# Three queues of a Mamba-like layer put in another order: SiLUs, squares and splits on ScalarE, GpSimd and VectorE

## What is computed

```python
proj = x @ Win.T                       # x is layer-normed
x_ssm, z, Bm, Cm, dt_raw = ...         # H*P, H*P, H*N, H*N, H columns
dt = softplus(dt_raw + dt_bias)
xc, Bc, Cc = (silu(causal_conv(u, w)) for u, w in ((x_ssm, wx), (Bm, wb), (Cm, wc)))
decay = exp(dt * -exp(A_log))
# for each token t: h = decay_t * h + (dt_t * xc_t) outer B_t;  y_t = h @ C_t
y = y * rsqrt(mean(y * y, axis=-1) + 1e-06)     # by head
y = y * silu(z)
return y.reshape(B, T, H * P) @ Wout.T
```

## Time and profile before

| | |
|---|---|
| median of three runs | 1110.2 us |
| the profiled execution | 1114.78 us |
| its span on the core | 1113.4 us |
| TensorE busy, matmuls | 1049.8 us (94%) |
| TensorE busy, weight loads | 870.7 us (78%) |
| VectorE busy | 777.2 us (70%) |
| GpSimd busy | 701.3 us (63%) |
| ScalarE busy | 610.5 us (55%) |
| granted TensorE clock, mean | 0.976 |

### The profile page before, as it was taken

One profiled execution on the slowest core, in us unless ns is written; L12 is line 12 of the kernel. 1 busy time (PEld: TensorE's weight loads), 2 busy tenths in 40 slices (PEclk: granted clock), 3 DMA queues, 4 the chain that ended last, 5 costly groups with the idle time before them and its releaser, 6 DMA issues.

```text
span 1113.4 us, 23878 instructions
## 1 busy us (share of the span) xinstructions
PE 1049.8 (94%) x9902; PEld 870.7 (78%) x9902; DVE 777.2 (70%) x1178; ACT 610.5 (55%) x945; POOL 701.3 (63%) x692
## 2 busy tenths in 40 slices
PE   8899999999999999999989999998888889999998
PEld 6678888888888888888877888886654578788887
DVE  5688887888878889788857446556758844655554
ACT  5877787777777767686715222225943533322221
POOL 3866786787867878676863667544447352365553
PEclk9999999999999999999999999999999979999999
DMA  3312111111111112101020643302131120233311
GB/s 108 109 68 77 48 61 64 60 57 67 58 49 67 53 63 73 41 32 48 1 68 3 227 134 101 118 1 67 43 94 28 29 64 3 94 129 100 121 65 39
DMA packets 47218, 75.97 MB, mean 68 GB/s; under 512 B 11330, under 2 KB 34150, under 8 KB 47110
## 3 DMA queue, kind: packets, MB, share of 16 engines
q1 hardware_dynamic: 47110, 74.44, 20.8%
HBM read 68.13 MB, written 2.36 MB: 63 GB/s over the span
## 4 chain that ended last, share of the span: by engine, by line
PE 63%; DVE 22%; ACT 6%; POOL 4%; issue 3%; DMA 1%; SPq 0%; DVEq 0%; POOLq 0%; ACTq 0%
PE psum L675 33%; PE psum L912 9%; DVE arena L1659 9%; PE psum L647 4%; DVE arena L1696 3%; PE psum L808 3%; PE psum L763 3%; PE psum L755 2%; PE psum L1021 2%; ACT arena L1201 1%; PE psum L985 1%; DVE arena L1919 1%; PE psum L1049 1%; PE psum L1033 1%; DMA vT<-arena 1%
## 5 line engine op out<-in xcount | busy, mean ns | idle before, releaser
L675 PE MATMUL psum<-vT,split 128*128 128x512 f32 x2136 | 542.7, 404 | 10.2 <-DVE arena L1659 5.5
L675 PEld LDWEIGHTS psum<-vT,split 128*128 128x128 f32 x2136 | 394.1, 191 | 100.9 <-DVE arena L1659 7.2
L1659 DVE SCALAR_TENSOR_TENSOR arena<-psum,arena 128x1023 f32<-128x1023 f32 (+2 forms) x208 | 265.6, 1277 | 80.5 <-ACT arena L1201 59.2
L2099 POOL TENSOR_TENSOR split<-arena,split 128x256 fp32r<-128x256 f32 x178 | 132.7, 759 | 65.1 <-ACT split L1126 64.9
L1201 ACT ACTIVATE arena<-psum,arena 128x512 f32<-128x512 f32 x160 | 109.4, 691 | 99.1 <-PE psum L675 98.2
L2306 POOL TENSOR_TENSOR arena<-arena,bcast 128x512 f32<-128x512 f32 x64 | 84.3, 1318 | 113.8 <-ACT arena L1370 97.3
L1370 ACT ACTIVATE arena<-psum,arena 128x512 f32<-128x512 f32 x72 | 49.7, 690 | 177.3 <-PE psum L675 177.2
L1809 DVE SCALAR_TENSOR_TENSOR arena<-psum,arena 128x512 f32<-128x512 f32 x72 | 53.9, 749 | 122.3 <-POOL arena L2306 117.3
L912 PEld LDWEIGHTS psum<-split_down,split_hid 128*128 128x128 f32 x864 | 114.9, 195 | 9.8 <-DVE split_hid L1822 3.2
L912 PE MATMUL psum<-split_down,split_hid 128*128 128x256 f32 x864 | 117.9, 287 | 2.5 <-DVE split_hid L1822 2.5
L2126 POOL TENSOR_TENSOR arena<-arena,v 128x1021 f32<-128x1021 f32 x32 | 76.4, 2389 | 46.9 <-DVE arena L1659 46.9
(11 more groups left out here) (217 smaller groups left out, 1540.2 us busy)
## 6 DMA issues: line engine op xcount, KB each, us to landing
bcast<-scratch_a SPq DMA_DIRECT2D x32, 512.0 KB, 3.6
bcast<-scratch_e SPq DMA_DIRECT2D x32, 512.0 KB, 4.2
arena<-in_w_a SPq DMA_DIRECT2D x16, 768.0 KB, 4.4
arena<-in_wg SPq DMA_DIRECT2D x36, 128.0 KB, 3.6
arena<-in_wu SPq DMA_DIRECT2D x36, 128.0 KB, 3.5
arena<-in_wd SPq DMA_DIRECT2D x36, 128.0 KB, 3.9
arena<-in_wout_a SPq DMA_DIRECT2D x8, 256.0 KB, 2.6
vT<-arena SPq DMA_DIRECT2D x2, 1024.0 KB, 5.3
```

Of the source, the lines that this page charges most:

```text
L675: m = pe.matmul(bank, split[:, t % SPLITS, i, q, :], vT[:, j, q, half * BANK:(half + 1) * BANK], start=(n == 0), stop=(n == 3 * KD - 1))
L1659: dve.scalar_tensor_tensor(out=tile[:, s:T], in0=bank[:, 0:T - s], scalar=cw_a[:, j, i, TAPS - 1 - s:TAPS - s], in1=tile[:, s:T], op0=ALU. ...
L2099: pool.tensor_tensor(split[:, t % SPLITS, 1], raw, split[:, t % SPLITS, 0].bitcast(F32), ALU.subtract).then_inc(sem["split"], 1)
```

## The change

Nothing is added or taken away; instructions move within three queues, all in the loop of layer (a).

ScalarE, body j: `silu(j, 4)`, which stood behind `first_tap(nxt, 0)` of body j, now stands at the end of the body before, as `silu(nxt, CONV - 1)`. `silu(nxt, 3)` moves ahead of `gate(nxt)`. `square(j)` stands at the end of body j, where `square(j - 1)` stood in the middle of body j. In odd bodies from 3 on, `gated_hi(j - 2)` stands ahead of `turned(j, 1, 1)`, and `wout_hi` ahead of `project_to(2)`. `silu(nxt, 0)` stands ahead of `turned(j, 1, 1)`. In body 0 the exponentials of `carries` come after `first_tap(1, 1)` and `silu(1, 0)` and not first.

VectorE: `sum_squares(j - 1)` stands after `mask(j, 0, 1)` and ahead of `taps(2, 1, 2)`, where it stood after `mask(j, 1, 1)`.

GpSimd: in odd bodies from 3 on, `wout_lo` stands right after `gated_lo`, ahead of `light(nxt, 1)` and the split of `project_to(2)`, where it stood behind them.

```diff
@@ ScalarE, scalar_program, first_layer @@
                             weights(TILES_A * nxt + i + SPLITS - 1)
                             first_tap(nxt, i)
-
-                    def silu_to(i):
-                        if nxt < PAIRS:
-                            silu(nxt, i)
-
-                    if j == 0:
-                        carries("a")
+                            if i in (2, 3):
+                                silu(nxt, i - 1)
+
                     project_to(0)
-                    if j:
-                        silu(j, CONV - 1)
                     turned(j, 0, 0)
                     turned(j, 0, 1)
                     turned(j, 1, 0)
-                    project_to(1)
+                    if nxt < PAIRS:
+                        weights(TILES_A * nxt + SPLITS)
+                        first_tap(nxt, 1)
+                    if j >= 3 and j % 2 == 1:
+                        gated_hi(j - 2)
+                    if nxt < PAIRS:
+                        silu(nxt, 0)
                     if j == 0:
+                        carries("a")
                         decays(0)
                     turned(j, 1, 1)
-                    if j >= 2:
+                    if j >= 2 and j % 2 == 0:
                         gated_hi(j - 2)
-                    silu_to(0)
-                    project_to(2)
-                    if j:
-                        square(j - 1)
                     if j >= 3 and j % 2 == 1:
                         wout_hi((j - 3) // 2)
-                    silu_to(1)
+                    project_to(2)
                     project_to(3)
-                    silu_to(2)
                     project_to(4)
                     if nxt < PAIRS:
                         decays(nxt)
                         weights(TILES_A * nxt + CONV + SPLITS - 1)
+                        silu(nxt, CONV - 2)
                         gate(nxt)
-                        silu(nxt, CONV - 2)
-                for g in range(2):
-                    square_head(PAIRS - 1, g)
+                        silu(nxt, CONV - 1)
+                        square(j)
+                    else:
+                        square_head(j, 0)
+                        square_head(j, 1)
@@ VectorE, vector_program, first_layer @@
                     mask(j, 0, 0)
                     mask(j, 0, 1)
+                    sum_squares(j - 1)
                     taps(2, 1, 2)
                     carry(j, range(0, 3))
                     taps(2, 3)
...
                     mask(j, 1, 0)
                     taps(3, 1)
                     mask(j, 1, 1)
-                    sum_squares(j - 1)
                     taps(3, 2)
@@ GpSimd, gpsimd_program, first_layer @@
                     if j >= 3 and j % 2 == 1:
                         gated_lo(j - 2)
+                        wout_lo((j - 3) // 2)
                     if nxt < PAIRS:
                         light(nxt, 1)
                     project_to(2)
-                    if j >= 3 and j % 2 == 1:
-                        wout_lo((j - 3) // 2)
```

## The result

Six runs of the changed kernel beside six of the kernel before gave a median of **1118.15 us** (1114.28 to 1119.98) against 1110.49; the ratio is 1.0056, with a 95% interval from 1.0028 to 1.0084. Twelve more runs beside another 29 of the kernel before gave 1116.65 against 1111.98, ratio 1.0032 (1.0010 to 1.0054). So the change costs 5 to 8 us in the medians.

A forecast was written before the change was run, and what follows sets the result against it. The prediction took TensorE to set the pace of the first layer's loop; 1.6 + 2.6 + 5 x 1.0 - 2.5 = +6.7 us, against a median of 1110.2, gave 1116.9 us, 0.6% more. The range was 1104 to 1124.

The forecast's parts named there:

- body 0: First loop body: carried products come 0 to 2.4 us later, but TensorE waits 2.40 us for VectorE soon after: zero.
- body 1: Second loop body: silu(1, 4) and square(0) add 1.9 us ahead of the first tap, the sum 1.1; net +1.6 us.
- bodies 2 and 3: Early loop bodies: no idle time before taps(2) in body 2, first tap 2.8 us late in body 3; together +2.6 us.
- last body: Body 15: TensorE's 2.87 us wait for normalize(14) goes, about 0.4 is lost again; gain 2.5 us.
- The odd bodies: Bodies 5, 7, 9, 11, 13: late first tap and early sum delay taps(2), so TensorE reaches inside(j, 0) 1.0 us later each.
- ScalarE's tail: End of a body: silu(nxt, 3) waits for light ahead of the gate; an odd body's first tap comes 1.4 us later.
- Even bodies: Loop's even bodies: first tap 0.9 to 1.8 us late, mostly taken in; the sum fits VectorE's idle 1.84 us; zero.
- rival 2: Even bodies at taps(2) pay too, up to 1.1 us in six bodies from 4 on; 1123.5 us; chance 0.15.
- rival 1: Odd bodies absorb the delay and only the gains stay, -5.5 us; 1104.7 us; chance 0.20.
- The sum's early place: End of body 8: GpSimd's normalize, no longer waiting for the sum, and light(9, 3) behind it end 1.4 us earlier.

The follow-up runs named there:

- e2: Kernel before with only VectorE's sum_squares(j - 1) early, behind mask(j, 0, 1), and ScalarE's square(j) at the body's end; 1114.26 us, ratio 1.0028.
- e5: Changed kernel with VectorE's taps(2, 3) moved behind all seven steps of the carry; 1107.53 us, ratio 0.9957 to the kernel before.
- e3: Changed kernel with sum_squares(j - 1) early only in even bodies from 4 on and the last body; 1111.16 us, ratio 1.0002 to the kernel before.
- e7: Changed kernel with sum_squares(j - 1) back behind mask(j, 1, 1) and gate(nxt) again ahead of silu(nxt, 3); 1118.10 us, ratio 1.0050 to the kernel before.
- e1: Changed kernel with only sum_squares(j - 1) put back behind mask(j, 1, 1); 1125.72 us, ratio 1.0135 to the kernel before.
- e9: Changed kernel with a second, unused 1.21 us reduction ahead of sum_squares(j - 1) in even bodies 4 to 14; 1118.35 us, ratio 1.0054 to the kernel before.
- e8: Kernel before with only body 0's two exponentials of ScalarE's carries moved after silu(1, 0); 1111.55 us, ratio 1.0001.
- e4: Kernel before with late carries in body 0, and sum_squares(j - 1) early in even bodies from 4 on and the last; 1102.10 us, ratio 0.9934.
- e6: Kernel before with late body-0 carries, early sum in even bodies from 4 and the last, taps(2, 3) behind the carry; 1099.94 and 1098.22 us.

## Why the prediction was right

| step | predicted | first traces | second traces |
|---|---|---|---|
| body 0, to the start of body 1 | 0 | -0.8 | -2.3 |
| body 1 | +1.6 | +1.4 | +1.4 |
| bodies 2 and 3, to `inside(3, 0)` | +2.6 | +2.5 | +2.5 |
| from there to the start of body 15 | +5.0 | +3.8 | +3.8 |
| last body | -2.5 | -3.4 | -3.3 |
| sum | +6.7 | +3.5 | +2.2 |

**The odd bodies.** The mechanism was the right one. The sum alone (e2) costs 0.87 in an odd body, the wait stands where it was put, even bodies stay at 0.53, and shortening the chain by 1.2 us takes 1.2 us off the wait (e5). Each odd body, with the tail before it, came to 0.83 us instead of 1.0. Five times that less the 0.3 at the end of body 14, which the sum had not counted, is the 3.8. The prediction's own terms give 1.1 and not 1.0 (1.42 of lateness less 1.24 and 0.15 of idle time, and 1.1 for the sum), so this term was too high by 0.3 each and not by 0.2.

**Bodies 1 to 3.** All three wait 1.4 us for the carry instead of 0.5. In body 3 the first tap comes 2.8 us late, counted from the start of body 2 (37.24 us behind it for 34.46), as worked out. What idle time doesn't take in stands not only at the carry, where the prediction had it: body 3 waits 0.53 us for `scale_u` and loses 0.3 ahead of product 2, and body 1 loses 0.28 and 0.3 there. The sizes (1.4 for 1.6, 2.5 for 2.6) came out right all the same.

**ScalarE's tail.** silu(nxt, 3) ahead of the gate does wait for `light` and the first tap is 1.7 us later against the transposes, where 1.4 was worked out on absolute times, with the 0.3 by which TensorE is earlier not in it: the same. That VectorE's idle time takes it in was right for the carry and incomplete for what stands before it. Product 2 waits for the end of taps(0), 0.2 us; the prediction had no term for this. e3, e7 and e1 show how close it was: without the sum a tap that is 1.70, 1.90 and 2.77 us late costs 0.33, 0.46 and 1.33.

**Even bodies.** Free, as said, with 0.71 us of cover left where 0.7 had been worked out; e9 showed the cover by using it up. So rival 2 didn't come, and rival 1 (the odd bodies absorb it) fell with the waits of 1.4 us and with e2.

**The sum's early place pays for the tail.** This the prediction said only in passing. Without the early sum the new order of ScalarE costs far more (e1, 1125.7). In the odd bodies this is because GpSimd's `normalize` and with it `light` come 1.1 to 1.4 us later; the larger part, 6.8 us, is the last body, where the waits for `normalize(14)` and turned(15, 1, 1) come back or grow. So the early sum of an even body covers the tail behind it, and in odd bodies it is the sum that costs.

**Last body.** The wait of 2.87 went as predicted. The term was too small since the clock also stayed up: the 24 products behind the wait took 2.95 us and not 4.09. Against this stand 0.36 and 0.27 us more for turned(15, 1, 1), which the prediction named, and 0.1 in front of `inside(15, 0)`; in front of `inside(15, 1)` it is 0.35 less.

**Body 0** was taken as zero because TensorE waits for VectorE afterwards. That was wrong: the chain of that wait moved too. With the exponentials out of the way the first tap and `scale_u(0, 1)` behind it come earlier, the wait of 2.15 us for `scale_u` goes, product 1 starts at 54.63 instead of 56.68 (second traces), and the wait for the carry falls from 2.41 to 0.53. The step of the prediction that failed is "TensorE waits 2.40 us for VectorE soon after, at 70.13: zero"; it took the start of the waiting chain as fixed. What showed in its place is 0.8 and 2.3 us less, and in e8 2.3 for this part alone, as long as the clock stays up behind the new wait.

**The total.** By the traces of the layer the sum of +6.7 us was 3.2 and 4.5 us too high; the medians (7.7 and 4.7 us) lie on both sides of it. That both medians come within 1.3 us of the forecast of 1116.9 is partly luck: the layer lost less and won more than predicted, and 2 us or so of the medians is not found in it.

## What to carry to other kernels

An instruction moved within a queue costs what the idle time in front of the next critical chain doesn't cover, and this differs between bodies of one loop: place it by body (here, early where VectorE has 1.8 us of idle time and late where it has 0.15) and not everywhere. Ask of each delay not only whether the last wait absorbs it but also who waits on the way. Ask of each wait whether the chain that ends it starts later or earlier with the same edit. A term measured in one body is not added to the next one unseen: the body behind may take a delay back (e9).

## What the runs showed of the hardware

- TensorE's granted clock fell behind some waits and not behind others of the same length. In all three traces with ScalarE's carries first (the two of the kernel before, and e2), products behind the wait of 2.4 us at about 70 us went at the lower of its two levels, 1.2 GHz instead of 2.4: 28 matmuls of 128 x 64 took 1.64 us from start to start (69.83 to 71.47) instead of 0.92, and the granted clock of 64 to 74 us was 0.83.
- With late carries one wait of 2.7 to 3.1 us stands ahead of `states(0, 0)` instead. In four of these eleven traces the clock stayed at 1.00 behind it (second trace of the changed kernel, e8, e4 and the first of e6, waits of 3.06 to 3.09 us). In the other seven it fell to between 0.80 and 0.86 in at least one of the two windows of 10 us from 54 to 74 us: behind waits of the same 3.06 and 3.08 us in two (e5, e3), and behind shorter ones of 2.74 to 2.76 us in all five that have such a wait. So the length of the wait alone doesn't tell it, and nothing here shows what does.
- What a wait costs is not only its length. At the end of the layer a wait of about 2.9 us was followed by 24 products in 4.09 and 4.45 us in the two traces of the kernel before, in 4.44 in e1 and 3.81 in e8, against 2.95 in the changed kernel: 0.9 to 1.5 us more. In e7, behind a wait of 2.86 us, they took 2.96, and nothing was added.
- The mean granted clock of identical executions lies between 0.969 and 0.990. In 24 runs of the kernel before the span went from 1105.2 us (at 0.990) to 1114.8 us (at 0.978). For differences below 1%, one profiled execution can hide the whole change, as it did here.
